# A fused four-level network on one core: TensorE's step order in attention, the place of the mask's product, and the times of one level's roundings

## The reference

```python
q, k = _rope(q, k)
scores = jnp.einsum('bqhd,bkhd->bhqk', q, k) / np.float32(np.sqrt(HEAD_DIM))
causal = jnp.tril(jnp.ones((S, S), bool))
scores = jnp.where(causal[None, None], scores, jnp.float32(-1e+30))
attn = jax.nn.softmax(scores, -1)
o = jnp.einsum('bhqk,bkhd->bqhd', attn, v)
x = x + o @ wo
```

## Time and profile before

| What | Value |
|---|---|
| median of 3 runs | 3796.96 us (3794.91 to 3799.11) |
| the profiled execution | 3797.79 us, of which the span is 3795.8 us |
| TensorE busy over the span | 3275.2 us (86%) |
| VectorE, ScalarE, GpSimd busy | 2467.2, 1972.1, 1694.4 us |
| level 0's attention, about 105 to 395 us | 290 us |
| level 2's attention, twice, about 1050 to 1712 and 2487 to 3157 us | 1330 us |

### The profile page before, as it was taken

The page is one execution under the profiler, slowest core; times in us unless marked ns, Lnnn a source line. Parts: engine busy times, 40 slices in busy tenths (PEclk is TensorE's granted clock), DMA queues, the critical chain, the costliest instruction groups (busy, mean ns, idle before and its releaser), DMA issues. The chain is left out here.

```text
span 3795.8 us, 55139 instructions
## 1 busy us (share of the span) xinstructions
PE 3275.2 (86%) x16736; PEld 2538.9 (67%) x16736; DVE 2467.2 (65%) x4877; ACT 1972.1 (52%) x3957; POOL 1694.4 (45%) x1293
## 2 busy tenths in 40 slices
PE   5778699569888889988996899888889987998979
PEld 4566577138666666666884799756666666886767
DVE  4668545765578778885556565368778885555554
ACT  3777443333367667774333333267667774334333
POOL 1666221652276666762221454267666662221111
PEclk8999899899999999999998899899999999999989
DMA  2000131433211111103320000010111102332222
GB/s 76 23 30 2 50 116 62 125 109 113 76 26 25 28 31 30 27 7 110 108 93 21 6 1 1 29 39 25 25 28 30 30 9 93 113 105 86 70 95 75
DMA packets 81187, 204.07 MB, mean 54 GB/s; under 512 B 17179, under 2 KB 20379, under 8 KB 80662
## 3 DMA queue, kind: packets, MB, share of 16 engines
q1 hardware_dynamic: 80774, 200.74, 17.1%
q10 hardware_dynamic: 144, 0.07, 0.0%
HBM read 170.86 MB, written 4.69 MB: 46 GB/s over the span
## 5 line engine op out<-in xcount | busy, mean ns | idle before, releaser
L1252 POOL TENSOR_TENSOR probs<-probs,row_inverse 128x640 f32<-128x640 f32 (+7 forms) x640 | 739.0, 1159 | 514.5 <-DVE row_inverse L1278 503.0
L541 PE MATMUL psUp<-xnT_part,weights_part 128*128 128x512 f32 x3456 | 834.7, 391 | 3.3 <-DVE hidden L694 2.6
L541 PEld LDWEIGHTS psUp<-xnT_part,weights_part 128*128 128x128 f32 x3456 | 651.6, 189 | 141.7 <-issue 4.0
L518 POOL TENSOR_TENSOR weights_part<-weights,weights_part 128x768 fp32r<-128x768 f32 x136 | 250.9, 1848 | 1010.2 <-ACT weights_part L597 1010.2
L1266 DVE TENSOR_REDUCE neg_max<-psS 128x1 f32<-128x640 f32 (+7 forms) x640 | 477.0, 745 | 143.5 <-PE psS L1156 141.4
L1293 DVE TENSOR_TENSOR probsT_part<-psT,probsT_part 128x512 fp32r<-128x512 f32 (+1 forms) x960 | 501.9, 550 | 78.0 <-ACT probsT_part L1235 68.9
L1219 ACT ACTIVATE probs<-psS,neg_max 128x640 f32<-128x640 f32 (+7 forms) x640 | 475.6, 743 | 144.5 <-DVE neg_max L1266 127.7
L1235 ACT ACTIVATE probsT_part<-psT 128x512 fp32r<-128x512 f32 (+1 forms) x960 | 441.0, 491 | 174.0 <-PE psT L1168 164.4
L1189 PE MATMUL psO<-probsT_part,v_parts 128*128 128x512 f32 x1440 | 443.0, 423 | 73.7 <-DVE probsT_part L1293 72.7
L1152 PE MATMUL psS<-k_part,q_parts 128*128 128x512 f32 (+1 forms) x960 | 410.6, 428 | 80.3 <-ACT probs L1219 45.1
L1168 PE MATMUL psT<-ident,probs 128*128 128x128 f32 x2880 | 439.0, 276 | 43.1 <-DVE probsT_part L1293 39.3
(11 more groups left out here) (315 smaller groups left out, 4825.6 us busy)
## 6 DMA issues: line engine op xcount, KB each, us to landing
gates<-gate_rows SPq DMA_DIRECT2D x136, 512.0 KB, 4.0
weights<-in_l_ffn SPq DMA_DIRECT2D x148, 384.0 KB, 4.4
qk_swapped<-qk_raw SPq DMA_DIRECT2D x384, 64.0 KB, 2.0
bc_broadcast<-bc_rows SPq DMA_DIRECT2D x32, 512.0 KB, 4.5
w_group<-in_l_wgroup SPq DMA_DIRECT2D x16, 384.0 KB, 3.2
q_whole<-q_steps SPq DMA_DIRECT2D x32, 128.0 KB
w_o_group<-in_l_wo SPq DMA_DIRECT2D x16, 256.0 KB, 2.8
rope<-in_l_rope SPq DMA_DIRECT2D x2, 1024.0 KB, 5.3
```

What stands on the lines that cost most here:

```text
L518: nc.gpsimd.tensor_tensor(w[1][:, j, :], wt[:, j, :], w[0][:, j, :].bitcast(F32), ALU.subtract).then_inc(w_split, 1)
L541: last = nc.tensor.matmul(psU[:, u % 2, g, :], wp[:, j, g * D + k * P:g * D + (k + 1) * P], xp[:, k, cols(half)], start=n == 0, stop=n == ...
L1252: self.nc.gpsimd.tensor_tensor(self.p[:, n % 4, 0:w], self.p[:, n % 4, 0:w], self.rinv[:, at:at + 1].to_broadcast([P, w]), ALU.mult).then_ ...
```

## The change

Three edits. In TensorE's step the values come ahead of the turns (both levels). In the scores of a diagonal chunk the mask's product comes behind the second product of the keys and closes the accumulation. In level 0 the roundings of pieces 0 to 3 move from steps 4, 4, 6, 12 to 13, 13, 14, 15, GpSimd's splits of pieces 0, 2, 3 from 6, 8, 14 to 14, 15, 16, and VectorE's split of piece 1 from 6 to 14. No instruction is added or removed.

```diff
             for b in range(qt // 4 + 1):
                 out = self.psS[:, n % 2, b, :]
                 w = min(max((qt + 1) * P - b * HALF, 2 * P), HALF)
+                diagonal = b == qt // 4
                 nc.tensor.matmul(out[:, 0:w], queries, keys[0][:, b * HALF:b * HALF + w], start=True, stop=False)
-                if b == qt // 4:
-                    diagonal = out[:, qt % 4 * P:(qt % 4 + 1) * P]
-                    nc.tensor.matmul(diagonal, self.ident16[:], self.mask16[:], start=False, stop=False)
                 done = nc.tensor.matmul(out[:, 0:w], queries, keys[1][:, b * HALF:b * HALF + w],
-                                        start=False, stop=True)
+                                        start=False, stop=not diagonal)
+                if diagonal:
+                    done = nc.tensor.matmul(out[:, qt % 4 * P:(qt % 4 + 1) * P], self.ident16[:], self.mask16[:],
+                                            start=False, stop=True)
             done.then_inc(self.scored, 1)
@@
         def step(g, s, last):
             scores(g, s + 8, last)
+            values(g, s, last)
             turn(g, s + 4, last)
-            values(g, s, last)
             self.hooks.pe_step(pe, g, s, last)
@@ class L0Hooks
-    ROUND_AT = {4: (0, 1), 6: (2,), 12: (3,), 20: (4,), 22: (5,)}
-    SPLIT_AT = {6: 0, 8: 2, 14: 3, 22: 4, 24: 5}
-    FIRST_KEYS_AT = 6
+    ROUND_AT = {13: (0, 1), 14: (2,), 15: (3,), 20: (4,), 22: (5,)}
+    SPLIT_AT = {14: 0, 15: 2, 16: 3, 22: 4, 24: 5}
+    FIRST_KEYS_AT = 14
```

## The result

The changed kernel takes 3930.52 us (median of 4 runs, 3926.05 to 3945.71) beside 3797.37 us for the kernel before on the same chip: a ratio of 1.0358 (95% interval 1.0329 to 1.0388), 133 us slower. The forecast was 3840, 43 us slower, with a range of 3765 to 3885; the sign was right, the size a third of what came, and the measured time lies outside the range and beyond the highest of the rivals (3880). Lines of the kernel after: keys' products L1153 and L1154, mask L1157, turn L1169, values L1190, exponential L1220, copy of half of `psO` L1228, copy of a bank L1236, split L1294.

The account below looks back on a forecast made before the run. TensorE was taken to lead, losing what it idles: 3797.8 us + 21 (level 0) + 54 (level 2) for the order, - 2 filled waits - 17 mask - 13 tables = 3841, forecast as 3840 us; range 3765 to 3885.

Parts of the forecast that it names:

- late chain: Values ahead of the turn at s % 4 = 2 delay ScalarE's copies, VectorE's join and the last split: 41 us.
- Uncovered turn at s % 4 = 0: The turn no longer fills TensorE's wait ahead of a quad's first values and is done later: 34 us.
- the last split is later, so the values at s % 4 = 0 start later: Put-off turn at s % 4 = 2 delays the quad's last split; in level 0's 4-block quad 0.54 of 0.81 us come through.
- banks too: Rival: at s % 4 = 3 turns also wait for banks not yet empty, +40 us, 3880 us; chance 0.14.
- The 2 us gained at s % 4 = 1: Values first fill the few waits ahead of turns at s % 4 = 1 and 2: about 2 us gained in all.
- the slow clock behind level 0's long wait: After ScalarE's 6.25 us wait for keys in level 0, TensorE is granted 0.50 of its clock for 4 us.
- Mask's product: Scores of diagonal chunks: mask last hides the second keys' load, 0.03 us in each of 640 units, -17 us.
- the rival in which it gave its bound of 58 us: Rival: scores' earlier end or the mask's load pulled ahead gains 58 us, 3799 us; chance 0.08.
- Tables: Level 0's later roundings remove ScalarE's two waits for keys and the slow clock behind: -13 us, bounds -8 and -15.
- its clock there stays at 1.00: Sign: in level 0, with ScalarE's wait for keys gone, the clock stays at 1.00.
- Turns as the true waits: Rival: values cost nothing ahead and fill the waits ahead of turns in both levels, 3728 us; chance 0.06.
- The 6-block quad's 1263.8 against 1262.8: Level 2's 6-block quad: end of first values and turn in the new order against before, given as +1.08 us.

Follow-up runs that it names:

- e4_mask_tables: Mask's product behind the second keys' product and level 0's moved roundings and splits, turns still ahead of values, against the kernel before: 3769.15 us, ratio 0.9927.

## Why the prediction was off

The measured time lies outside the forecast's range and above every rival. Two steps failed: a term was missing (TensorE's busy time), and the late chain came out at another place than the one it was worked out for.

- **Uncovered turn at s % 4 = 0.** Right in mechanism and in size as idle time (34 forecast, 32 measured). Its cost of 56 us holds 24 more of busy time.
- **Late chain at s % 4 = 2.** As idle time again near in sum (41 forecast, 35 measured), but by luck of the place: the step "the last split is later, so the values at s % 4 = 0 start later" is the one that failed. Taken alone, the edit leaves the waits ahead of values as they were. The late turn holds ScalarE's exponential, and the scores wait for that; it also makes the turn at s % 4 = 3 wait for a bank, as the rival "banks too" had it (32 waits with 17.9 us in a stage of level 2, against 9 with 10.9). That rival's time of 3880 was nearer, but it priced these waits at 40 us where they are 7 us in each stage of level 2.
- **The 2 us gained at s % 4 = 1.** Wrong: TensorE loses 16 us there in idle time, 30 us in all. The late turn at 1 makes the turn at 2 wait for banks (5.8 us in a stage of level 2 against 0.8).
- **The term that was missing.** The sum was made of idle time alone, 73 us. TensorE's busy time rose by 81 us between e4_mask_tables and the changed kernel: by estimate 41 by the granted clock, 17 by the ends of products ahead of 105 more waits, some 11 by what the mask's product no longer saves, and 12 that I can't place. The prediction had priced the slow clock behind level 0's long wait and didn't ask the same of its own new waits.
- **Mask's product.** Forecast -17, alone -12, but in the new order nothing. The two edits were priced as if they didn't meet; the load that follows the mask is another one once the values come next. The mask's load still follows 0.28 us idle, and the rival in which it gave its bound of 58 us is refuted.
- **Tables.** Forecast -13, measured -13 alone. ScalarE has no wait for the keys' DMA left in level 0 of the changed kernel. With the order, against the order alone, the tables bring 7 us, within the intervals of both. The sign "its clock there stays at 1.00" came true only around these waits (1.00 from 200 to 216 us): the new order's waits bring the clock down elsewhere in level 0, to 0.82 from 224 to 232 us, for example.
- **Turns as the true waits.** Refuted: the turns wait more, not less.
- **Slips in the working.** The 6-block quad's 1263.8 against 1262.8 is 1.0 us and not 1.08, and half of the 0.22 for "no change" is 0.11 and not 0.14. Neither moves the forecast.

Measured against the forecast's sum: +21 + 54 - 2 became +134, -17 became about +7, -13 about -7.

## What to carry to other kernels

Price a new wait twice: the idle time itself, and what TensorE's clock does behind it. If an edit brings new waits close together, look in the rows of granted clock for stretches at half speed; here that was some 40 of 133 us, by estimate. A wait also adds the end of the last product to the busy time, so compare busy time and number of waits as well as idle time. In a ring of engines, follow a late result to every engine that handles something else behind it in order (here ScalarE's exponential), not only along its own data. And price edits that touch neighbouring instructions together, since what hides a weight load is the product ahead of it.

## What the runs showed of the hardware

- Behind waits of 0.60 and 1.59 us, with three products between them, the granted clock fell from 1.00 to 0.66 in the next window of 4 us; from 1480 us on these are the only ones of over 0.15 us ahead of the fall. Products added for nothing into such waits made the kernel faster, or at least no slower: 68 us of busy time for a change of -11 us in the median.
- The bf16 weight load of the mask's product, 0.10 us long, is not pulled ahead of a running product: in the changed kernel, where it stands last, all 320 such loads behind a product of 384 or 512 columns follow at least 0.15 us without any load (median 0.26 us), as most did between two products in the kernel before (288 of 320, median 0.22). Behind a product of 256 columns it follows 0.04 us without a load.
